# Node numbers for the block factors and the attention's one-hots read from PSUM, and block factors ahead of a slot's add

## The reference

```python
x = layernorm(x + L0(x))   # sum over edges of x[src], weighted by one of 16 relations, 2 bases
x = layernorm(x + L1(x))   # two such passes over the edges, 32 relations, 4 bases, tanh
x = layernorm(x + L2(x))   # relu(sum over edges of x[src] @ W.T + b)
x = layernorm(x + L3(x))   # 8-head attention over the edges: softmax of q[dst].k[src] per target
```

## Time and profile before

| | |
|---|---|
| median of 3 runs | 2023.86 us (2019.08 to 2028.87) |
| profiled execution | 2026.14 us, its span 2024.3 us |
| POOL, DVE, PE busy | 1440.2, 1555.9, 1611.5 us |
| layer 0, gathers | 5 to 533 us |
| layer 1, gathers | 544 to 953 us |
| layer 2, gathers | 968 to 1371 us |
| attention, gathers | 1459 to 1992 us |

### The profile page before, as it was taken

One profiled execution on the slowest core, in us unless ns is written; L12 is line 12 of the kernel. 1 busy time (PEld: TensorE's weight loads), 2 busy tenths in 40 slices (PEclk: granted clock), 3 DMA queues, 4 the chain that ended last, 5 costly groups with the idle time before them and its releaser, 6 DMA issues.

```text
span 2024.3 us, 36062 instructions
## 1 busy us (share of the span) xinstructions
PE 1611.5 (80%) x10129; PEld 1326.4 (66%) x10160; DVE 1555.9 (77%) x4756; ACT 1070.8 (53%) x2202; POOL 1440.2 (71%) x1482
## 2 busy tenths in 40 slices
PE   3988888888589888898399999997628777677777
PEld 2766776667477777777387877774417656566666
DVE  7886767767679888898477777777859877777786
ACT  3355646555588677666466655552464343434341
POOL 6777777777577777776677777772277777777772
PEclk9566566665699999999699999999855555555555
DMA  6232232323133333433534343432286555555551
GB/s 184 56 89 78 66 89 56 88 57 88 51 103 100 104 105 103 132 103 88 155 76 131 111 134 105 130 105 90 85 222 175 162 169 154 163 158 161 161 147 45
DMA packets 171435, 231.75 MB, mean 114 GB/s; under 512 B 48220, under 2 KB 123983, under 8 KB 170980
## 3 DMA queue, kind: packets, MB, share of 16 engines
q0 software_dynamic: 53376, 123.02, 22.0%
q1 hardware_dynamic: 116710, 104.76, 17.5%
q10 hardware_dynamic: 1154, 1.67, 0.3%
HBM read 196.52 MB, written 36.08 MB: 115 GB/s over the span
## 4 chain that ended last, share of the span: by engine, by line
PE 20%; POOL 18%; issue 7%; DVE 6%; DMA 3%; ACT 2%; SPq 1%; DVEq 0%; POOLq 0%; ACTq 0%
POOL G L2021 17%; PE p_d L944 4%; PE p_d L873 4%; PE p_g L931 4%; PE p_g L815 3%; DMA G<-kv_d,idx 2%; PE p_o L858 2%; DMA G<-h_d,idx 1%; POOL G L748 1%; DVE hs L2281 1%; PE p_w L2081 1%; SPq L694 1%; ACT agg L1215 1%; PE p_o L853 1%; DVE XH L2275 0%
## 5 line engine op out<-in xcount | busy, mean ns | idle before, releaser
L748 POOL DMA_INDIRECT G<-h_d,idx x624 | 619.9, 993 | 217.9 <-issue 179.5
L2021 POOL DMA_INDIRECT G<-kv_d,idx x416 | 405.1, 974 | 162.6 <-issue 158.0
L748 POOL DMA_INDIRECT G<-in_x,idx x416 | 400.5, 963 | 131.4 <-issue 111.2
L815 PEld LDWEIGHTS p_g<-S,G 128*128 128x128 f32 x2080 | 352.9, 233 | 163.9 <-issue 96.3
L815 PE MATMUL p_g<-S,G 128*128 128x96 f32 (+1 forms) x2080 | 372.4, 314 | 102.2 <-DMA G<-in_x,idx 56.9
L1404 DVE SCALAR_TENSOR_TENSOR S<-con,rel,shared 128x96 f32<-128x96 f32 (+1 forms) x1040 | 262.3, 294 | 0.4
L1182 ACT ACTIVATE work<-con,lo_f 128x128 bf16<-128x128 f32 x416 | 143.1, 392 | 206.7 <-PE p_d L827 206.6
L1431 DVE TENSOR_TENSOR agg<-agg,p_g 128x96 f32 (+1 forms) x520 | 119.7, 230 | 158.9 <-PE p_g L815 143.1
L944 PE MATMUL p_d<-Sb,kv_s 128*128 128x288 f32 x728 | 220.2, 420 | 20.6 <-ACT kv_s L1174 13.2
L1522 DVE TENSOR_TENSOR work<-work,p_d 128x312 f32 (+1 forms) x416 | 180.2, 465 | 58.1 <-PE p_d L827 52.1
L2081 PE MATMUL p_w<-oh,PV 128*128 128x40 f32 x832 | 195.1, 410 | 24.4 <-DVE PV L2334 23.2
(11 more groups left out here) (338 smaller groups left out, 2950.9 us busy)
## 6 DMA issues: line engine op xcount, KB each, us to landing
dst_b<-in_dst_row SPq DMA_DIRECT2D x104, 240.0 KB, 3.2
work<-A_d SPq DMA_DIRECT2D x25, 800.0 KB, 5.7
A_d<-work SPq DMA_DIRECT2D x12, 1600.0 KB
G<-h_d,idx POOLq DMA_INDIRECT x624
G<-in_x,idx POOLq DMA_INDIRECT x416
kv_s<-low_d SPq DMA_DIRECT2D x52, 128.0 KB
G<-kv_d,idx POOLq DMA_INDIRECT x416, 3.3
kv_s<-low_d SPq DMA_DIRECT2D x52, 96.0 KB
```

The lines of the kernel that those rows point to most:

```text
L748: pool.indirect_dma_start(G[:, n % GRING, :], None, l.table, bass.IndirectOffsetOnAxis(ap=l.places[:, c:c + 1], axis=0)).then_inc(s_arr[i ...
L815: last = pe.matmul(p_g[:, g % PB, 0:width], G[:, c % GRING, :], S[:, c % (SRING * GR), 0:width], start=(k == 0), stop=(k == GR - 1))
L2021: pool.indirect_dma_start(G[:, c % KRING, :], None, d["kv"], bass.IndirectOffsetOnAxis(ap=idx[:, c:c + 1], axis=0)).then_inc(s_arr[c // QC ...
```

## The change

The block factors read the node numbers from PSUM: 73 numbers are copied once into columns 432 to 504 of both banks `p_g[0]` and `p_g[1]`, beyond the columns that `sums` writes. Because a bank mustn't be read while PE writes it, `own_numbers` picks the bank of group `i-3`, waits for that group's matmuls, and the block factors of slot `i` now stand ahead of the slot's `add`. The attention's one-hots read their 40 numbers from free columns of the bank `p_bk`, copied once per sweep. The computed values are the same.

```diff
+I_AT = 432
-        def block_factor(l, m):
+        def own_numbers(slot):
+            if slot >= 2:
+                dve.wait_ge(s_mm, max(slot - 2, 1))
+            return p_g[:, max(slot - 3, 0) % PB if slot >= 2 else slot]
+
+        def block_factor(l, m, numbers):
             i, k = m // GRP, m % GRP
             if m >= SBR:
                 dve.wait_ge(s_bs2, m - SBR + 1)
             f, row = l.f0 - 2, slots[:, i, k, :]
             dve.scalar_tensor_tensor(Sb[:, m % SBR, 0:l.nb * WB].rearrange("p (b w) -> p b w", w=WB),
-                                     bc(con[:, C_I + 1:C_I + 1 + WB], 1, l.nb), row[:, PAY - 2:PAY - 1],
+                                     bc(numbers[:, I_AT + 1:I_AT + 1 + WB], 1, l.nb), row[:, PAY - 2:PAY - 1],
                                      bc(row[:, f:f + l.nb], 2, WB), ALU.is_equal, ALU.mult).then_inc(s_Sb, 1)
...
             for i in range(-LEAD, l.end):
                 if l.n == 0 and (s := step_at(i + 10)) is not None:
                     coef_eq(s)
+                for m in buckets_at(l, i + 1):
+                    block_factor(l, m, own_numbers(i))
                 if 0 <= i - 3 < l.ng:
                     add(l, i - 3)
...
                 if 0 <= i < l.ng:
                     factors(l, i)
-                for m in buckets_at(l, i + 1):
-                    block_factor(l, m)
...
-        dve.wait_ge(s_lay, 2)
+        for k in range(PB):
+            dve.tensor_copy(p_g[:, k, I_AT:I_AT + WB + 1], con[:, C_I:C_I + WB + 1]).then_inc(s_lay, 1)
+        dve.wait_ge(s_lay, 2 + PB)
...
+    numbers = p_bk[:, P:P + WA]
...
+            dve.tensor_copy(numbers, iota).then_inc(s_lay, 1)
+            dve.wait_ge(s_lay, 9)
...
-                dve.tensor_tensor(oh1[:, k % OH1, j * QC:(j + 1) * QC, :], bc(iota, 1, QC),
+                dve.tensor_tensor(oh1[:, k % OH1, j * QC:(j + 1) * QC, :], bc(numbers, 1, QC),
                                   bc(rel[:, c:c + QC], 2, WA), ALU.is_equal).then_inc(s_oh1, 1)
```

More of the change, by code:

```diff
@@ L1859, in vector @@
         dve.memset(itc[:], 0.0).then_inc(s_lay, 1)
-        dve.wait_ge(s_lay, 3)
+        dve.wait_ge(s_lay, 3 + PB)
         with dve.Fori(0, iterations(dve, L[2])):
@@ L2260, in sweep_start @@
             dve.tensor_copy(R0[0:1, 1, :, CB], fut[0:1, 1, :, 1]).then_inc(s_lay, 1)
-            dve.wait_ge(s_lay, 8)
+            dve.tensor_copy(numbers, iota).then_inc(s_lay, 1)
+            dve.wait_ge(s_lay, 9)
         def one_hots(k):
```

## The result

The changed kernel takes **2002.75 us** (median of 4 runs, 2000.6 to 2006.43) against 2023.87 before: ratio 0.9896, 95% interval 0.9877 to 0.9915. Beside the last experiments it was timed again: 2000.64 us (6 runs, 1998.27 to 2001.90), ratio 0.9890, interval 0.9873 to 0.9908. The forecast was 2001. The profiled execution took 2000.6 us with a span of 1998.8.

What follows compares the result with a forecast made beforehand. POOL's gathers were taken to pace the attention and, closely followed by DVE and PE, layer 1; PE paced layer 2. Terms -9.3 - 12 - 4 + 2 + 0.3 = -23.0 gave 2003.1, less 2.3 to the median: 2001 us, range 1989 to 2015.

Steps and rivals of the forecast that it cites:

- What stretches a gather: POOL's gathers: DVE instructions with both tensor inputs in SBUF hold them; excess 18.2 us layer 1, 12.6 layer 2, 12.4 attention.
- The rival that the broadcast inputs hold them: One-hots and block factors: their broadcast inputs, not where these lie, hold gathers; 2026 us, chance 0.05.
- Attention, -9.3: Attention's one-hots: numbers in PSUM end 9.3 us of gather stalls, all arriving at the end; bounds 0 and -12.4.
- Layer 1, -12 between -5 and -15.9: Layer 1's block factors: POOL regains 15.9 us, counted only as far as PE waited for gathers; -12 us taken.
- Layer 2, -4: Layer 2's block factors: POOL regains 8.1 us, but PE waited 3.9 for gathers; -4 us, between 0 and -8.1.
- a sign that the forecast is wrong: PE's waits for `add`: growth by 10 us or more would show the forecast wrong.
- The length of the instructions, 0: Block factors and one-hots on DVE: -22 to +3 ns each with numbers from PSUM; taken as 0.
- The rival of longer instructions: Layer 1's block factors on DVE: 66 ns more each from PSUM cancels 12 us; 2013 us, chance 0.05.
- Place and second wait, +2 between -4 and +8: Block factors ahead of `add`: about 15 us of new DVE waits, mostly in slack; +2 us.
- The rival that ended slower: The wait for block sums holds `add` and PE's next group in every block; 2051 us at 2 us a block, chance 0.06.
- The rival in which the sum layers give it all back: Layers 1 and 2: PE and DVE become the bound once gathers come faster; 2012 to 2014.6 us, chance 0.16.

Runs made afterwards that it cites:

- e4: Changed kernel with block factors back behind `S`, numbers from the PSUM bank of group i-2, waiting for that group's matmuls; 2015.34 us, ratio 0.9952.
- e10: e4 with the same place and waits, but block factors reading their numbers from SBUF; 2020.9 us, ratio 0.9991.
- e1: Kernel before with only the attention's one-hots reading their numbers from PSUM; 2014.19 us, ratio 0.9947.
- e7: Kernel before with each step's four one-hots issued at separate places, still with two SBUF inputs; 2019.19 us, ratio 0.9973.
- e2: Changed kernel with the attention's one-hots reading their numbers from SBUF again; 2012.07 us, ratio 0.9938.
- e6: Changed kernel with layer 2's block factors reading their numbers from SBUF again; 2001.06 us, ratio 0.9884.
- e3: Kernel before with only the block factors moved ahead of the slot's add, numbers still in SBUF; 2024.02 us, ratio 0.9998.
- e5: Changed kernel with each block's second block sum of slot 10 moved to slot 11; 1998.8 us, ratio 0.9875.

## Why the prediction came out

*What stretches a gather.* Right, and now shown: the same gathers under the same instructions are no longer stretched once one input is in PSUM. The rival that the broadcast inputs hold them falls, since they are still broadcast. The cleanest pair is e4 and e10, which differ only in where the numbers lie: with all waits the same, POOL's excess in layer 1 is 3.5 us with the numbers in PSUM and 13.8 with them in SBUF. The Trainium skill (SBUF — State Buffer, Who interferes with whom) has the general rule that two SBUF inputs contend with GpSimd's reads and at most one doesn't, and the runs agree. It also says that an old probe didn't see `tensor_tensor` stalling a DMA; there the runs differ, by e1's 10.1 us, for the one-hots are TENSOR_TENSOR.

*Attention, -9.3.* Measured -10.1 by the medians of e1, -8.8 in the traces. Right, and all of it arrived, as it should where POOL is the pace to the end.

*Layer 1, -12 between -5 and -15.9.* The pair of traces gives -15.3. But the stretch varies: with stalls and the old place it is 423.5, 420.5 (e1) and 423.9 (e7), without them and with the changed kernel's order it is 408.2, 409.6, 409.3 (e2) and 406.8 (e6). The means are 422.6 and 408.5, 14.1 us. Two more traces have the stalls and are shorter: 418.7 with the new place (e3) and 417.8 with e10's waits, 10.2 us above the mean of 408.5 and 9.1 above e4. One reason is that it is chance how many gathers meet a block factor: their excess in layer 1 is 15.9 us before, 12.9 in e1, 17.0 in e7, 11.2 in e3 and 11.0 in e10. The prediction counted it in one trace, the second highest of the five. By the medians of e2 all that the block factors bring is 12.3. So the mechanism was right and -12 lies within what the traces give, 9 to 15. But the way from 15.9 to 12 isn't borne out: it counted the saving only up to PE's last wait for a gather, while the pair of traces has all 15.0 us of the gathers in the layer's length. The gathers came without a pause to their end, and what followed them stayed 16 us long. PE's waits for gathers fell below 8, as said.

*Layer 2, -4.* This is the step that was mis-sized: 0, and e6 shows it. I had counted the 3.9 us of PE's waits for gathers as time won. They went (none is left), but PE's wait for `add` took their place: "issue" in front of the sums went from 1.1 to 8.5 us. A wait of PE was removed that had another right behind it. In layer 1 the same "issue" went from 0.6 to 10.3 us, so together it grew by 17 us, and the prediction had named 10 us or more of it as a sign that the forecast is wrong. The sign came and the forecast held: this wait stood where one for gathers had stood, and so it isn't a loss by itself. The prediction's own reading, that PE is the pace there, should have put this term at 0.

*The length of the instructions, 0.* 514 to 509 ns and 307 to 304 ns, some 2 us of DVE in all. The rival of longer instructions falls. By the figures of the Trainium skill (VectorE: DVE Perf Modes, The TRN2 errata) a PSUM source would cost an estimated 65 ns more; neither form here bears this out.

*Place and second wait, +2 between -4 and +8.* Measured by e3, without the second wait: -0.3, between -2.4 and +1.8. The second wait was not run by itself; but DVE's waits for the group's matmuls were 43.7 us before, all at `add`, and are 44.2 now, 39.5 at the block factors and 4.7 at `add`, so it brought nearly none that `add` didn't have. DVE got 11.1 us more of waits for block sums (11.1 to 22.2), where 15 were said, and in layer 2 they cost nothing that e5 could show: without them the wait for the group's matmuls is longer by nearly as much. The rival that ended slower rested on this wait holding `add`. That waits of DVE can cost time there is shown by e10, whose stricter wait for group i-2 costs 8 us; the wait for the block sum in slot 9 costs no such amount.

*The sum.* -4 for layer 2 against 0, and +2 for the place against 0, cancel within 2 us, and so the forecast of 2001 hit both measurements, 2002.75 and 2000.64, better than its terms deserve. That closeness is luck; the mechanism and the two large terms are not. The rival in which the sum layers give it all back, 2012 to 2014.6, was true of layer 2 and not of layer 1.

## What to carry to other kernels

Where gathers on GpSimd pace a stretch, look for the ones longer than the median and see which DVE instruction ends 0.8 us before they do: putting one of its two inputs into PSUM gave back all of the excess that hung on it here, and merely breaking up a run of such instructions more than half. An excess counted in one trace is a sample: here it came out between 11 and 17 us in five kernels whose block factors read SBUF. Count the gain only in stretches where that engine is the pace to their end; where another is, it bought a different wait here, and the layer stayed as long. The operand's new home has to be free at the instruction's place: ahead of `add` the bank's wait was one that `add` made anyway, behind `S` the stricter one cost 8 us by itself, more than a third of the gain.

## What was not expected of the hardware

The stall lasts to the end of an unbroken run of instructions: four one-hots back to back held 18 gathers for 9.3 us, 0.52 us each, and apart they held 23 for 3.8, 0.16 us each. A TENSOR_SCALAR of 600 elements from f16 to bf16 (L1508, 0.52 us), whose only tensor input is in SBUF, was under way from 0.06 us ahead of the start of 96 gathers of the kernel before to 0.15 us after it, and none of them took more than 0.96 us. And the granted clock of PE fell in e4 three times in the middle of layer 2 to 0.50 for some 3 us each, in 260 us of which PE was busy for 96%; one of the falls follows pauses of 1.5 us within 6 us, and over the layer the clock took 3.7 us more than in e10.
